# Who combines the expert rows in the last stage of a decoder layer: a different split over ScalarE, GpSimd and VectorE

## The reference

```
top_vals, top_idx = jax.lax.top_k(logits, 2)
gates = jax.nn.sigmoid(top_vals)
...
gu = x @ gate_up_w[e];  h = silu(gate) * up;  y_e = h @ down_w[e]
moe = sum over the two experts of a token of gates * y_e
x = x + moe + shared
```

## Time and profile before

| what | us |
|---|---|
| three runs | 569.35, 568.07, 563.98 |
| median | 568.07 |
| the profiled execution | 568.54 |
| its span, first to last instruction | 566.7 |
| VectorE busy in the span | 409.6 (72%) |
| ScalarE busy | 296.8 (52%) |
| GpSimd busy | 298.4 (53%) |
| TensorE busy | 469.9 (83%) |

### The profile page before, as it was taken

The page is one execution under the profiler, slowest core; times in us unless marked ns, Lnnn a source line. Parts: engine busy times, 40 slices in busy tenths (PEclk is TensorE's granted clock), DMA queues, the critical chain, the costliest instruction groups (busy, mean ns, idle before and its releaser), DMA issues. The chain is left out here.

```text
span 566.7 us, 17496 instructions
## 1 busy us (share of the span) xinstructions
PE 469.9 (83%) x6139; PEld 348.1 (61%) x6139; DVE 409.6 (72%) x1247; ACT 296.8 (52%) x757; POOL 298.4 (53%) x588
## 2 busy tenths in 40 slices
PE   1977888888888888888999999999767999999810
PEld 1755666666666666545676676666544888888610
DVE  7566999999888888876889898987572434434337
ACT  2573665555556656524656656564424444444237
POOL 5543454444444334201358888777771577777720
PEclk9997999999999999969999999999989999999975
DMA  6626343455655655326233333332124334333158
GB/s 189 112 51 139 55 71 63 67 132 111 110 108 110 108 107 114 81 52 150 54 83 90 95 87 97 96 85 67 34 97 132 106 110 116 110 109 98 53 178 286
DMA packets 96006, 58.30 MB, mean 103 GB/s; under 512 B 24560, under 2 KB 92224, under 8 KB 95920
## 3 DMA queue, kind: packets, MB, share of 16 engines
q1 hardware_dynamic: 74448, 39.93, 30.2%
q10 hardware_dynamic: 16896, 7.34, 6.7%
q0 software_dynamic: 4576, 9.91, 5.1%
HBM read 20.76 MB, written 17.50 MB: 68 GB/s over the span
## 5 line engine op out<-in xcount | busy, mean ns | idle before, releaser
L507 POOL TENSOR_SCALAR veps<-mv 128x2 f32<-128x2 f32 x48 | 11.2, 232 | 144.9 <-issue 101.2
L1292 ACT ACTIVATE probs<-ps 128x512 f32<-128x512 f32 x128 | 73.3, 603 | 12.1 <-PE ps L1672 9.8
L613 POOL DMA_INDIRECT expert_in<-xn,sloti x64 | 65.5, 1023 | 17.6 <-issue 17.6
L1147 DVE TENSOR_TENSOR eh<-ps,sg 128x256 f32<-128x256 f32 x40 | 17.0, 425 | 59.8 <-ACT sg L1496 58.9
L772 DVE TENSOR_REDUCE nmax<-ps 128x8 f32<-128x512 f32 x64 | 42.5, 686 | 18.9 <-PE ps L1607 18.8
L666 POOL DMA_INDIRECT expert_out<-ey,xt x40 | 38.3, 957 | 27.0 <-DVE ey L1154 16.7
L772 DVE TENSOR_REDUCE mparts<-ps 128x8 bf16<-128x512 f32 x64 | 43.3, 687 | 6.7 <-PE ps L1662 6.3
L1607 PE MATMUL ps<-kbd,qs 96*64 96x128 bf16 x512 | 38.0, 293 | 4.5 <-DMA qs<-part 3.6
L2026 PE MATMUL ps<-wgu,turned 128*128 x160 | 41.3, 380 | 0.0
L1490 ACT COPY turned<-ps 128x512 f32<-128x512 f32 (+1 forms) x43 | 23.8, 554 | 28.5 <-PE ps L2019 23.2
L509 POOL TENSOR_TENSOR rstd<-veps,minus_half 128x2 f32<-128x2 f32 x48 | 35.8, 745 | 4.0
(11 more groups left out here) (248 smaller groups left out, 1360.2 us busy)
## 6 DMA issues: line engine op xcount, KB each, us to landing
kbd<-part SPq DMA_DIRECT2D x192, 32.0 KB
qs<-part ACTq DMA_DIRECT2D x93, 64.0 KB
xt<-expert_in SPq DMA_DIRECT2D x64, 72.0 KB
qs<-part SPq DMA_DIRECT2D x51, 64.0 KB
ck_scr<-wgu SPq DMA_DIRECT2D x6, 512.0 KB
ckbd<-ck_scr SPq DMA_DIRECT2D x16, 192.0 KB
kbd<-part SPq DMA_DIRECT2D x48, 64.0 KB
wgu<-in_L_ffn_gate_up_w SPq DMA_DIRECT2D x4, 512.0 KB, 4.0
```

The source lines that it names most:

```text
L613: pool.indirect_dma_start(xs, bass.IndirectOffsetOnAxis(sloti[b % 3][:, n:n + 1], 0), xn3[b % 3][:, n // TOPK, n % TOPK, :], None).then_in ...
L1292: a_.activation(probs[:, 2 * i:2 * i + 2, :], P2[i % 2][:, :].rearrange("p (j q) -> p j q", j=2), ACT.Exp, scale=SCALE).then_inc(s("probs" ...
```

## The change

`ALONE` goes from three batches to six, 0, 1, 4, 7, 10 and 13, so that ScalarE gates ten batches instead of thirteen. For these ten, GpSimd adds the two gated rows of a token (`y[k=0] += y[k=1]`, 128x256 f32) when ScalarE has gated all four rows, and VectorE adds the sum to x in one instruction instead of two. A new semaphore `paired` counts GpSimd's adds. The six batches alone are combined as before. VectorE waits for the end of its own reciprocal before the first batch. In the self-attention stage the keys' copy counts on `kgqg` instead of on a semaphore of its own, and the waits are renumbered: `headed(b)` = 3b+2.

```diff
-        ALONE = (3, 8, 13)
+        ALONE = (0, 1, 4, 7, 10, 13)
+
+        def paired(b):
+
+            return b + 1 - sum(a <= b for a in ALONE)
...
+        def headed(b):
+
+            return 3 * b + 2
...
-                last.then_inc(s_("kbg"), 1)
+                last.then_inc(s_("kgqg"), 1)
...
-                pool.wait_ge(s_("kgqg"), 2 * b + 4)
+                pool.wait_ge(s_("kgqg"), headed(b + 1))
...
                 step_loop(pool, rows_out, 0)
+
+                def paired_rows(b):
+
+                    y = yrow[b % BACK][:, :, :].rearrange("p (u k) c -> p u k c", k=TOPK)
+                    pool.wait_ge(g_("scaled"), 2 * TOPK * paired(b))
+                    g.tensor_tensor(y[:, :, 0, :], y[:, :, 0, :], y[:, :, 1, :], ALU.add).then_inc(g_("paired"), 1)
+
+                for b in range(B):
+                    if b not in ALONE:
+                        paired_rows(b)
...
-                                dve.wait_ge(g_("first"), b + 2 + ALONE.index(b))
+                                dve.wait_ge(g_("first"), 2 * ALONE.index(b) + 2)
...
-                    dve.wait_ge(g_("scaled"), 2 * TOPK * (b + 1 - sum(a < b for a in ALONE)))
-                    v.tensor_tensor(xb, xb, y[:, :, 0, :], ALU.add).then_inc(g_("first"), 1)
-                    dve.wait_ge(g_("first"), b + 1 + sum(a < b for a in ALONE))
-                    v.tensor_tensor(xb, xb, y[:, :, 1, :], ALU.add).then_inc(g_("x_out"), 1)
+                    dve.wait_ge(g_("paired"), paired(b))
+                    v.tensor_tensor(xb, xb, y[:, :, 0, :], ALU.add).then_inc(g_("x_out"), 1)
...
                 v.reciprocal(gate[:, :], gate[:, :]).then_inc(r_("plan"), 1)
+                dve.wait_ge(r_("plan"), PLANNED + 4)
...
-                at_least(act, s_("kgqg"), 2 * b - 2)
+                at_least(act, s_("kgqg"), headed(b - 2))
...
-                pe.wait_ge(s_("kgqg"), 2 * b + 2)
+                pe.wait_ge(s_("kgqg"), headed(b))
...
-                pe.wait_ge(s_("kbg"), b + 1)
+                pe.wait_ge(s_("kgqg"), headed(b) + 1)
```

## The result

The changed kernel takes 569.42 us (median of 20 runs, 567.99 to 572.64), the kernel before 567.63 in 20 runs beside it (563.98 to 570.85). The ratio is 1.0041, with a 95% interval from 1.0023 to 1.0059: 1.3 to 3.3 us slower, 2.3 in the middle.

What follows compares the result with a forecast made beforehand. VectorE was taken to decide the last stage: from 553.1, adds 3.1, batches alone 4.9, last instruction's end 0.1 and GpSimd collisions 4.0 make 12.1, ending at 565.2, 0.8 us later than before; forecast 569.0 us, range 565.8 to 572.0.

Steps and rivals of the forecast that it cites:

- Two thirds of ScalarE's relief worth nothing: Last stage: ScalarE loses three batches, 3.5 us, but removing batches 0 and 1 moves nothing, as it still starts batch 2 at 549.86.
- GpSimd's add at 0.722: Last stage: each of GpSimd's ten 128x256 f32 adds takes 0.722 us, taken from its bias add; ends 0.612 and 1.303.
- 0.8 to 1.0 where it is not: Last stage: GpSimd's adds take 0.72 us where VectorE is idle and 0.8 to 1.0 us where VectorE is not idle.
- The turns: Last stage: VectorE and GpSimd alternate on SBUF reads; each GpSimd add arriving in VectorE's stream costs VectorE 505 ns.
- rival 2: Last stage: each GpSimd add costs VectorE its whole 0.72 us, 5.8 instead of 4.0; about 571 us; chance 0.15.
- Eight turns: VectorE's stream: GpSimd's adds of batches 5, 6, 8, 9, 11, 12, 14, 15 cost 0.505 us each, 4.0 in all.
- the latency of 3.2 us: Last stage: the load of batch 15 goes out at 558.6 and takes 3.2 us, landing at about 561.9.
- the sum's 565.2: VectorE from 553.1: nine adds 3.1, four batches alone 4.9, last instruction's end 0.1, GpSimd collisions 4.0; 12.1 us, ending at 565.2.
- The last add: End of VectorE's work in the last stage: 565.2 against 564.44, so 0.8 us later.
- Edits at nothing: Keys' copy counting on the heads' semaphore and the wait after the reciprocal: no wait ends at another moment, no cost.
- Rival 1: Last stage: no collision of GpSimd and VectorE; ScalarE and transfers bound, last add at 564.1, 568.2 us; chance 0.20.
- Rival 3: Last stage: GpSimd's add takes 1.3 us or more, last add at 570.2 or beyond, 574.3 us in all; chance 0.05.

## Why the prediction was right, and where it wasn't

- The time. I said 569.0 us, 0.8 more than before on the same execution, within 1%. Measured 569.4 and 2.3 more, within 1%. The direction and the kind of loss were right, the size a third of the measured one. That 569.0 and 569.4 lie so close is luck: the kernel before came out 0.4 us lower in twenty runs than in the three that I started from, which hides part of the missing 1.5.
- Two thirds of ScalarE's relief worth nothing: right. With the batches 0 and 1 gone it starts batch 2 when their rows land, as the idle time in the earlier trace rows said.
- GpSimd's add at 0.722: right where it is undisturbed (0.72). The sign "0.8 to 1.0 where it is not" held for four of six.
- The turns: right in kind, and the price of 505 ns from one pair of rows in another stage held: the long instructions lose 0.35 to 0.55 us, 0.47 on average. Writing without reading made them vanish. Of rival 2, the full 0.72 per turn, none of them shows anything. The Trainium skill says (SBUF — State Buffer, "Who interferes with whom") that a GpSimd instruction which only writes doesn't contend with VectorE's two SBUF inputs; the 24 fused instructions at 345 to 352 ns agree. The same section calls the shared ports "an exclusive lock"; read as the prediction did, as a block for the whole of the other's instruction, that is more than was lost, 0.35 to 0.55 us against an add of 0.72.
- Eight turns: six came. The other two, for batches 14 and 15, fell into holes, because their rows were late. The prediction let the load of batch 15 land at 18.1 us after SP's first load, "nothing else is later"; it landed at 18.9. The step that failed is the latency of 3.2 us for loads that go out late: the load of batch 15 went out at 14.7, as forecast, and took 4.2, and that of batch 14, which ScalarE waited for, took 4.29. I had seen that the queue was full before, and had not asked what late loads do to it. With sixteen buffers all eight came. There the sum's 565.2, which is 21.4 on the clock of before, measured 20.8: 0.2 of the difference is an earlier add of batch 3, 0.2 the turns at 0.48 instead of 0.505, and 0.2 I can't place.
- The last add: forecast 0.8 later, measured 1.0. The nearness is luck: two of the eight turns didn't come, and late loads that the sum didn't have took their place.
- The missing term: "2.3 us follow the last add, so the whole forecast is: where does the last add end?" and "nothing is queued behind" GpSimd's adds. The end of the program is queued behind them. GpSimd's drain takes 3.6 us after its last instruction, whichever that is; in the kernel before it was over 20 us before the end. It is 1.1 us of the 2.1. That it ends the kernel is shown alone (1.0039, and 4.0 us behind the last add) and by taking it away (2.3 us again).
- Edits at nothing: right (0.9992).
- Rival 1, no collision, would have had all fused instructions at 0.346; five of 24 weren't. Rival 3 had adds of 1.3 us; the longest was 1.02.

## What to carry to other kernels

Work given to GpSimd at the end of this program was paid for twice: by what it took from VectorE, and by the end of the program on GpSimd. Look up in the profile when each engine's last instruction ends and how long its drain follows, before giving it the last piece. And whatever lengthens the instructions of the engine that gives buffers back delays the loads, too: where transfers are the near second bound, ask what a late load costs.

## What the runs showed of the hardware that I had not expected

- GpSimd's drain at the program's end came 3.6 us after its last instruction in five kernels, whether this was a scatter, an add, a memset of 0.58 us or one of 0.10 us. In the kernel before, VectorE's drain took 0.46 us, SP's 13 ns. Why GpSimd's takes so long no run here shows.
- After the late loads the transfers were slow for a while: for three microseconds they moved 239 GB/s instead of 335 to 339, and a load took 4.29 us where 2.9 is possible from an idle start. The start of the stage has such a dip too, 141 GB/s from 547 to 548 in the kernel before. That the queue had nearly emptied is a guess, and why the transfers are slow then was not tried.
